# A cross-attention layer on one core: loads, roundings and query projections of the opening in another order

## The chip, the cores and the metric

The kernel runs on one core of one Trainium2 chip. The metric is the device time of one execution in microseconds, median of the runs. Before the change it is 512.16 us (three runs: 514.06, 511.97, 512.16).

## The reference, cut to what matters

```python
x = x + xattn(layernorm(x), ctx, mask)      # 128 queries, 12544 keys, 16 heads of 16, D = 256
x = x + attn(layernorm(x))                  # causal self-attention over the 128 rows
x = x + ffn(layernorm(x))                   # quantised gated MLP, 256 -> 768 -> 256

# xattn:
qh = (q @ Wq.T + bq).reshape(B, 128, 16, 16)
kh = (k @ Wk.T + bk).reshape(B, 12544, 16, 16)
vh = (v @ Wv.T + bv).reshape(B, 12544, 16, 16)
scores = einsum('bqhd,bkhd->bhqk', qh, kh) / 4
scores = where(mask, -1e7, scores)          # the mask of this case is all False
out = einsum('bhqk,bkhd->bqhd', softmax(scores), vh)
```

## The kernel before

The context has 14 blocks of 896 keys. A first phase (until about 243 us) goes through the blocks once: it projects keys and values, writes them to scratch in HBM, and finds each query's largest score. A second phase (until about 480 us) reads keys and values back, forms scores, exponentials and weighted sums. Self-attention and the MLP follow. The change is in the opening, the first 25 us or so, before the first phase has its rhythm.

Every fp32 operand of a key or value projection is kept as two parts, a rounded one and the rest: `ctx_hi` and `ctx_lo`, `w_hi` and `w_lo`. A projection is three products (hi x hi, hi x lo, lo x hi), each over two chunks of D: 6 matmuls for half a block of keys of one 128-row chunk (L815), 12 for two value tiles (L824).

Every engine has a program of its own, and their order is written by hand; semaphores tie them together. The parts that matter here:

- SyncE (SP) issues the loads one after another (L232 to L254): x, context block 0, Wk, Wv, the unit matrix `eye`, `wqn`, `bqn`, `head_mask`, `causal`, `bk`, and `mask_all`, the whole attention mask (1568 KB, L242). Then it waits until context block 0 is split, loads context block 1 into the same buffer (L245), and issues eight small loads for `bqr` and `row_mask` (L248 to L251), then `bv`, `wqvk`, `wo`, and the stores and loads of the block loop (L263, L265, L259).
- ScalarE (ACT) rounds context block 0 (L413, L414), spreads Wq's columns four-fold (L418, three copies), then evacuates keys (L427) and values (L433) in the order of the projections. Between two of these it rounds the next context block (L405), at position 5 of block 0 and position 3 of block 1. Later it also copies scores (L440, L443).
- VectorE (DVE) does the layer norm of x, rounds Wk and Wv into `w_hi` (L573), copies the turned rows (L567), forms `w_lo` (L575) and half of `ctx_lo` (L579), takes the projected queries out of PSUM (L595), forms `k_lo` of the first half block (L589), and writes `q_pad` (L599): for each of the 16 heads the 128 queries with all rows but this head's zeroed. Then `k_lo` of the second half, the maximum over the whole mask (L608), the flag "is anything masked" (L610), three casts of small matrices (`big_eye`, `eye_b`, `causal_b`, L612 to L614), four small steps on `row_mask` and `bqr` (L616 to L620), and `qr`, the spread queries with their bias (L621), which raises `q_copied`.
- GpSimd (POOL) forms the other half of `ctx_lo` (L359), issues two loads of mask rows (L356), fills `k_stack` with ones (L365), splits block 1 (L349, four pieces), waits for `q_copied`, and makes `q_stack` out of `qr` in eight operations (L370 to L377). Only then comes its share of block 2 (L349 again). SP loads a block into the single context buffer only after POOL has split the one before (L258, L259).
- TensorE (PE) first runs 14 matmuls on zeros (L867), then: transposes of x (L875), queries (L881), projections 0 and 2 of block 0, then 4 and 6 (`slot` counts in steps of two: keys 0/0, values 0, keys 0/1, values 1), the spread queries (L893, 32 matmuls into PSUM banks 2 and 3), the one-column sum of the flag (L898). It reads the flag (L900), branches (L1122), waits for `q_ready` and `q_copied` (L904, L905), and goes on with slot 8; from there every slot has a projection and one step of scores (L856).

```python
            pe.wait_ge(flag_ready, 1)
            masked_flag = pe.value_load(flag_i[0:1, 0:1], min_val=0, max_val=1)
            ...
                pe.wait_ge(q_ready, 1)
                pe.wait_ge(q_copied, 1)
```

The scores of step u go to banks 0 and 1 and, for even u, 2 and 3, for odd u, 4 and 5.

Of the kernel before, what the change touches and what calls it, by code (L numbers as in the profile page):

```python
# [4 lines left out]
H = 16  # L5
HD = 16
D = H * HD
Q = 128
SK = 12544
F = 768  # L10
P = 128
DC = D // P
# [34 lines left out]
WARM_FIRST = 14  # L47
# [4 lines left out]
def perceiver_layer(nc: bass.Bass, x_d, ctx_d, maskn_d, maskt_d, wqn_d, wqr_d, bqn_d, bqr_d, wk_d, bk_d, wv_d, bv_d,  # L52
# [9 lines left out]
    with ExitStack() as stack_of_contexts:  # L62
# [5 lines left out]
        def sem(name):  # L68
# [27 lines left out]
        q_pad = sb("q_pad", [P, H, Q], f32r)  # L96
# [33 lines left out]
        small = sb("small", [P, 16])  # L130
        magic = sb("magic", [P, 2])
# [98 lines left out]
        def _(sp):  # L230

            sp.dma_start(x0[:], x_d).then_inc(x_in, 16)  # L232
            sp.dma_start(ctx_t, ctx_d[0]).then_inc(ctx_in, 16)
            sp.dma_start(w_kv[:, 0:DC * D], wk_d.rearrange("p c n -> p (c n)")).then_inc(wkv_in, 16)
            sp.dma_start(w_kv[:, DC * D:], wv_d.rearrange("p c n -> p (c n)")).then_inc(wkv_in, 16)
            sp.dma_start(eye[:], eye_d).then_inc(eye_in, 16)
# [14 lines left out]
            sp.dma_start(row_mask[SLOTS::STRIDE, 2:4], pairmask_d[0:2 * HD, :]).then_inc(rows_in, 16)  # L251
            sp.dma_start(bv[:], bv_d).then_inc(bv_in, 16)
# [48 lines left out]
            sp.wait_ge(w_split, 1)  # L301
# [30 lines left out]
        def _(pool):  # L332
# [69 lines left out]
        def _(act):  # L402
# [11 lines left out]
            nc.scalar.copy(ctx_hi[:, 0, 1, :], ctx_t[:, BK:2 * BK]).then_inc(ctx_hi_ready, PIECES)  # L414
            act.wait_ge(wqn_in, 16)
# [29 lines left out]
            def evacuate(s, par, first, last=False):  # L445
# [3 lines left out]
                for slot, work in enumerate(PROJECTIONS):  # L449
# [92 lines left out]
        def _(dve):  # L542
# [22 lines left out]
            def copy_turned(nth, psum):  # L565
# [6 lines left out]
            dve.wait_ge(wkv_in, 32)  # L572
            link(nc.vector.tensor_copy(w_hi[:, :, :, :].rearrange("p w c n -> p (w c n)"), w_kv))  # L573
            copy_turned(1, ps_a[:, 0, 0:D])
            nc.vector.tensor_tensor(w_lo[:, :, :, :].rearrange("p w c n -> p (w c n)"), w_kv,  # L575
                                    w_hi[:, :, :, :].rearrange("p w c n -> p (w c n)").bitcast(f32),
                                    ALU.subtract).then_inc(w_split, 1)
            dve.wait_ge(ctx_hi_ready, 1)
            nc.vector.tensor_tensor(ctx_lo[:, 0, 1, :], ctx_t[:, BK:2 * BK], ctx_hi[:, 0, 1, :].bitcast(f32),  # L579
                                    ALU.subtract).then_inc(low_context, 1)  # L580
            dve.wait_ge(bq_in, 16)
# [10 lines left out]

            dve.wait_ge(q_projected, 1)
            for m in range(DC):
                link(nc.vector.tensor_scalar(x3[:, m * Q:(m + 1) * Q], ps_a[:, 1, m * Q:(m + 1) * Q], bqn[:, m:m + 1],  # L595
                                             HD ** -0.5, ALU.add, ALU.mult))
            low_keys(0, 0, 0, 0)
            for m in range(DC):
                last = nc.vector.tensor_tensor(  # L599
                    q_pad[:, m * HT:(m + 1) * HT, :],  # L600
                    x3[:, m * Q:(m + 1) * Q].unsqueeze(1).to_broadcast([P, HT, Q]),
                    head_mask[:, :].unsqueeze(2).to_broadcast([P, HT, Q]), ALU.mult)
# [582 lines left out]
```

## Time and profile before

| | us |
|---|---|
| median of three runs | 512.16 |
| the profiled execution | 513.95 |
| its span, first to last instruction | 512.2 |
| PE busy | 484.1 (95%) |
| ACT busy | 375.8 (73%) |
| DVE busy | 294.8 (58%) |
| POOL busy | 101.1 (20%) |
| mean granted TensorE clock | 0.966 of full speed |

Times in the profile count from the start of the span; 1.75 us of the profiled execution lie outside it. In the rows below, PE is matmuls and PEld weight loads; an engine's name with a q (SPq, PEldq) is its queue or sequencer. A weight load or matmul has the two halves of its name, out and in. Granted clock 1.00 is 2.4 GHz and 0.50 is 1.2 GHz.

### The profile page before, as it was taken

How to read it: one execution, taken by the hardware profiler on the slowest of the kernel's cores; microseconds unless marked ns; L12 is line 12 of the kernel's file. 1: busy time of each engine (PE TensorE's matmuls, PEld its weight loads, DVE VectorE, ACT ScalarE, POOL GpSimd, SP SyncE). 2: the span in 40 equal slices, each digit the busy share in tenths (PEclk: the TensorE clock that was granted, in tenths of full speed). 3: DMA queues.
4: the chain of work that ended last, by engine and by line, in shares of the span. 5: the costliest groups of instructions: out<-in, count | busy, mean ns of one | idle time of the engine just before them, and what ended most of it. 6: DMA issues, size and time to landing. Idle time of an engine off the chain costs nothing.

```text
span 512.2 us, 14299 instructions
## 1 busy us (share of the span) xinstructions
PE 484.1 (95%) x5643; PEld 380.3 (74%) x5643; DVE 294.8 (58%) x427; ACT 375.8 (73%) x411; POOL 101.1 (20%) x101
## 2 busy tenths in 40 slices
PE   6889999999999999996999999999999999989897
PEld 3867776777776777774489998999989999859443
DVE  6757999999999999999759600000000000046575
ACT  4347888888888788876389889899898999925011
POOL 5684322333322333304000000000000000000000
PEclk8879999999999999998799999999999999998799
DMA  8735776665776656985957788777677778000000
GB/s 275 262 123 210 284 282 267 236 233 229 300 289 257 242 219 240 388 349 213 385 188 288 302 309 307 275 252 274 259 268 271 273 292 312 3 2 1 0 0 14
DMA packets 34760, 117.47 MB, mean 229 GB/s; under 512 B 4401, under 2 KB 10417, under 8 KB 34737
## 3 DMA queue, kind: packets, MB, share of 16 engines
q1 hardware_dynamic: 30560, 110.58, 56.8%
q0 software_dynamic: 4032, 6.42, 4.4%
q8 instruction: 17, 0.28, 0.2%
q10 hardware_dynamic: 144, 0.13, 0.1%
q14 instruction: 7, 0.05, 0.0%
HBM read 74.44 MB, written 39.47 MB: 222 GB/s over the span
## 4 chain that ended last, share of the span: by engine, by line
PE 61%; DVE 22%; issue 8%; ACT 5%; DMA 2%; POOL 1%; DVEq 0%; SPq 0%; ACTq 0%; POOLq 0%
PE ps_a L953 20%; PE ps_k L967 18%; DVE block_max L628 10%; PE ps_k L815 6%; DVE early L631 5%; PE ps_a L824 4%; PE ps_a L856 3%; ACT early L443 3%; PE ps_k L867 2%; DMA early<-in_ctx 1%; DMA v_in<-in_wv 1%; DVE k_lo L589 1%; PE ps_a L1039 1%; PE ps_a L1054 1%; PE ps_a L893 1%
## 5 line engine op out<-in xcount | busy, mean ns | idle before, releaser
L628 DVE TENSOR_REDUCE block_max<-ps_a 128x2 f32<-128x896 f32 x112 | 120.8, 1080 | 1.8 <-PE ps_a L856 1.7
L953 PE MATMUL ps_a<-q_stack,k_stack 128*128 128x256 f32 x784 | 110.1, 291 | 1.4 <-ACT middle L494 1.4
L953 PEld LDWEIGHTS ps_a<-q_stack,k_stack 128*128 128x128 f32 x784 | 98.3, 188 | 13.5 <-issue 11.6
L443 ACT CAST early<-ps_a 128x896 bf16<-128x896 f32 x104 | 94.0, 903 | 8.0 <-PE ps_a L856 8.0
L494 ACT ACTIVATE middle<-ps_a 128x1536 f32<-128x1536 f32 (+1 forms) x56 | 90.2, 1662 | 10.6 <-PE ps_a L953 10.6
L494 ACT ACTIVATE early<-ps_a 128x1536 f32<-128x1536 f32 (+1 forms) x56 | 90.2, 1662 | 7.8 <-PE ps_a L953 7.8
L691 DVE COPY early<-ps_k 128x256 f32<-128x256 f32 x2 | 0.8, 420 | 163.7 <-PE ps_k L967 163.7
L349 POOL TENSOR_TENSOR k_stack<-early,k_stack 128x448 fp32r<-128x448 f32 x52 | 59.2, 1143 | 122.6 <-DVE early L631 113.6
L824 PE MATMUL ps_a<-w_hi,k_stack 128*128 128x256 f32 x392 | 69.8, 301 | 0.0
L631 DVE TENSOR_TENSOR early<-early 128x896 bf16<-128x896 bf16 x104 | 67.6, 650 | 0.0
L815 PE MATMUL ps_k<-k_stack,w_hi 128*128 128x448 f32 x224 | 61.8, 398 | 6.1 <-DVE v_in L621 3.9
L824 PEld LDWEIGHTS ps_a<-w_hi,k_stack 128*128 128x128 f32 x392 | 54.6, 194 | 11.9 <-issue 11.8
L856 PE MATMUL ps_a<-k_hi,q_pad 32*128 32x448 f32 x448 | 54.5, 475 | 8.6 <-ACT early L443 7.7
L427 ACT ACTIVATE k_hi<-ps_k,bk 128x448 fp32r<-128x448 f32 x56 | 35.6, 635 | 31.6 <-PE ps_k L815 31.6
L815 PEld LDWEIGHTS ps_k<-k_stack,w_hi 128*128 128x128 f32 x224 | 38.7, 192 | 20.9 <-DVE k_lo L589 11.0
L967 PE MATMUL ps_k<-early,v_in 128*17 128x128 f32 x1568 | 48.4, 273 | 0.0
L967 PE MATMUL ps_k<-middle,v_in 128*17 128x128 f32 x1568 | 48.2, 273 | 0.0
L856 PEld LDWEIGHTS ps_a<-k_hi,q_pad 32*128 32x128 f32 x448 | 22.0, 186 | 35.0 <-issue 23.6
L589 DVE SCALAR_TENSOR_TENSOR k_lo<-ps_k,bk,k_hi 128x448 fp32r<-128x448 f32 x56 | 38.0, 678 | 13.3 <-ACT k_hi L427 10.8
L967 PEld LDWEIGHTS ps_k<-early,v_in 128*17 128x17 f32 x1568 | 40.4, 97 | 3.9 <-ACT early L494 0.3
L967 PEld LDWEIGHTS ps_k<-middle,v_in 128*17 128x17 f32 x1568 | 40.4, 97 | 3.8
L433 ACT COPY early<-ps_a 128x512 f32<-128x512 f32 (+1 forms) x56 | 30.1, 537 | 15.2 <-PE ps_a L824 12.9
(172 smaller groups left out, 434.7 us busy)
## 6 DMA issues: line engine op xcount, KB each, us to landing
k_stack<-k_hi_scratch SPq DMA_DIRECT2D x56, 448.0 KB, 6.1
v_scratch<-early SPq DMA_DIRECT2D x14, 952.0 KB, 6.1
v_in<-v_scratch SPq DMA_DIRECT2D x14, 952.0 KB, 8.1
early<-in_ctx SPq DMA_DIRECT2D x14, 896.0 KB, 5.6
k_hi_scratch<-k_hi SPq DMA_DIRECT2D x28, 448.0 KB, 3.3
k_lo_scratch<-k_lo SPq DMA_DIRECT2D x28, 448.0 KB, 3.7
k_stack<-k_lo_scratch SPq DMA_DIRECT2D x28, 448.0 KB, 6.1
mask_b<-in_maskn POOLq DMA_DIRECT2D x14, 224.0 KB, 5.6
```

Source lines behind the costliest of these rows:

```text
L349: nc.gpsimd.tensor_tensor(ctx_lo[:, par, c, half], ctx_t[:, c * BK:(c + 1) * BK][:, half], ctx_hi[:, par, c, half].bitcast(f32), ALU.subtr ...
L427: nc.scalar.activation(k_hi[:, par, m, n * HK:(n + 1) * HK], ps_k[:, 0:HK], ACT.Identity, bias=bk[:, m:m + 1]).then_inc(hi_ready, 1)
L443: nc.scalar.copy(staged[:, u % 2], pair_scores(u, 0)).then_inc(max_copied, 1)
L494: nc.scalar.activation(probs[u % SLOTS_P][:, 0:width], ps_a[:, UNIT_BANK[u % 2]:UNIT_BANK[u % 2] + UP[u % 2] // 2, :].rearrange("p a n -> ...
L589: nc.vector.scalar_tensor_tensor(k_lo[:, m, half], ps_k[:, 0:HK], bk[:, m:m + 1], k_hi[:, par, m, half].bitcast(f32), ALU.add, ALU.subtrac ...
L628: nc.vector.tensor_reduce(block_max[:, par, 2 * u:2 * u + 2], pair_scores(u, 1), AX.X, ALU.max).then_inc(max_taken, 1)
L631: nc.vector.tensor_tensor(copied_rows(u), copied_rows(u), staged[:, u % 2], ALU.max).then_inc(run_taken, 1)
L815: last = nc.tensor.matmul(ps_k[:, 0:HK], w[:, 0, c, m * P:(m + 1) * P], part[:, par, c, n * HK:(n + 1) * HK], start=(k == 0), stop=(k == l ...
L824: last = nc.tensor.matmul(ps_v[:, n * D:(n + 1) * D], part[:, par, c, t * P:(t + 1) * P], w[:, 1, c, :], start=(j == 0), stop=(j == len(te ...
L856: last = nc.tensor.matmul(outs[-1], q_pad[rows, head, :], k_hi[rows, par, m, keys], start=True, stop=not masked, skip_group_check=True)
L953: last = nc.tensor.matmul(ps_a[:, bank, (k % 2) * 2 * Q:(k % 2 + 1) * 2 * Q], k_stack[:, b_par, a, t * P:(t + 1) * P], q_stack[:, a, :, :] ...
L967: last = nc.tensor.matmul(attended[32 * j:32 * j + VW, c * Q:(c + 1) * Q], v_ring[:, b_par, t, h, :], probs[slot][:, k * Q:(k + 1) * Q], s ...
```

## The change

SP: `eye` is loaded second, and the context, Wk and Wv behind it; Wk and Wv have a semaphore each. `causal` goes behind `mask_all`. The eight small loads go ahead of context block 1, and block 1 waits for `mask_all` to have landed as well. POOL issues the two loads of mask rows after filling `k_stack`, not before.

ACT rounds Wk and Wv, each when it is there, and makes `big_eye`, `eye_b` and `causal_b` after the evacuation of values 0. DVE forms `w_lo` in two halves, behind its half of `ctx_lo`. `q_pad` (16 heads x 128) becomes `q_pair` (2 x 2 x 128), the queries times a mask of two columns, even heads and odd heads; the score matmuls read 32 rows of it, which hold one head of each parity. The flag's sum goes to bank 3, and the spread queries to banks 4 and 5. PE: 12 zero matmuls and 6 more behind the transposes; spread queries between slots 2 and 4; slot 6 behind the flag's sum; `q_copied` is waited for before score step 1 and not ahead of slot 8.

```diff
-WARM_FIRST = 14
+WARM_FIRST = 12
+WARM_OPEN = 6
 @block.sync
             sp.dma_start(x0[:], x_d).then_inc(x_in, 16)
+            sp.dma_start(eye[:], eye_d).then_inc(eye_in, 16)
             sp.dma_start(ctx_t, ctx_d[0]).then_inc(ctx_in, 16)
-            sp.dma_start(w_kv[:, 0:DC * D], ...).then_inc(wkv_in, 16)
-            sp.dma_start(w_kv[:, DC * D:], ...).then_inc(wkv_in, 16)
-            sp.dma_start(eye[:], eye_d).then_inc(eye_in, 16)
+            sp.dma_start(w_kv[:, 0:DC * D], ...).then_inc(wk_in, 16)
+            sp.dma_start(w_kv[:, DC * D:], ...).then_inc(wv_in, 16)
...
-            sp.dma_start(causal[:], causal_d).then_inc(masks_in, 16)
             sp.dma_start(bk[:], bk_d).then_inc(bk_in, 16)
             sp.dma_start(mask_all...).then_inc(mask_all_in, 16)
-            sp.wait_ge(ctx_split, PIECES)
-            sp.wait_ge(low_context, 1)
-            sp.dma_start(ctx_t, ctx_d[1]).then_inc(ctx_in, 16)
+            sp.dma_start(causal[:], causal_d).then_inc(masks_in, 16)
             sp.wait_ge(row_mask_clear, 1)
             (eight small loads of bqr and row_mask)
+            sp.wait_ge(ctx_split, PIECES)
+            sp.wait_ge(low_context, 1)
+            sp.wait_ge(mask_all_in, 16)
+            sp.dma_start(ctx_t, ctx_d[1]).then_inc(ctx_in, 16)
 @block.gpsimd
-            load_rows(0, 0, True)
-            load_rows(1, 1, True)
             for n, (fill, value) in enumerate(fills[-2:]):
                 ...
+            load_rows(0, 0, True)
+            load_rows(1, 1, True)
 @block.scalar
+            for part, arrived in enumerate((wk_in, wv_in)):
+                act.wait_ge(arrived, 16)
+                nc.scalar.copy(w_hi[:, part]..., w_kv[:, part * DC * D:(part + 1) * DC * D]).then_inc(w_high, 1)
...
                         evacuate_values(s, par, work[1])
+                        if first and par == 0 and work[1] == 0:
+                            act.wait_ge(eye_in, 16)
+                            act.wait_ge(masks_in, 32)
+                            nc.scalar.mul(big_eye[:], eye[:], BIG).then_inc(eyes_set, 1)
+                            nc.scalar.copy(eye_b[:], eye[:]).then_inc(eyes_set, 1)
+                            nc.scalar.copy(causal_b[:], causal[:]).then_inc(eyes_set, 1)
 @block.vector
             layernorm(x0[:]).then_inc(normed, 1)
-            dve.wait_ge(wkv_in, 32)
-            link(nc.vector.tensor_copy(w_hi[...], w_kv))
             copy_turned(1, ps_a[:, 0, 0:D])
-            nc.vector.tensor_tensor(w_lo[...], w_kv, w_hi[...], ALU.subtract).then_inc(w_split, 1)
             (its half of ctx_lo)
+            for part in range(2):
+                dve.wait_ge(w_high, part + 1)
+                nc.vector.tensor_tensor(w_lo[:, part]..., ALU.subtract).then_inc(w_split, 1)
             dve.wait_ge(bq_in, 16)
             dve.wait_ge(masks_in, 32)
+            link(nc.vector.tensor_reduce(parity_mask[:], head_mask... "p (j e) -> p e j", AX.X, ALU.max))
             dve.wait_ge(q_projected, 1)
             (two steps L595)
+            nc.vector.tensor_tensor(q_pair[...], x3 to [P, 2, D], parity_mask to [P, 2, D], ALU.mult).then_inc(q_ready, 1)
             low_keys(0, 0, 0, 0)
-            (q_pad, two multiplications of 128x1024, then_inc(q_ready, 1))
-            low_keys(0, 0, 0, 1)
             nc.vector.memset(row_max[:], LEAST)
             dve.wait_ge(mask_all_in, 16)
             nc.vector.tensor_reduce(flag_f[:], mask_all, AX.X, ALU.max).then_inc(flag_asked, 1)
+            dve.wait_ge(rows_in, 16 * 2 * STRIDE)
+            (the scaling of bqr)
             dve.wait_ge(flag_summed, 1)
+            (flag_i, out of bank 3).then_inc(flag_ready, 1)
-            (big_eye, eye_b, causal_b; the wait for rows_in)
+            low_keys(0, 0, 0, 1)
+            dve.wait_ge(q_projected, 2)
             (three steps on row_mask, then qr).then_inc(q_copied, 1)
 @block.tensor
+                if isinstance(s, int) and s * NG + u == 1:
+                    pe.wait_ge(q_copied, 1)
...
             last.then_inc(transposed, 1)
+            keep_clock(ps_v, WARM_OPEN)
...
-            pe.wait_ge(w_split, 1)
             pe.wait_ge(ctx_split, PIECES)
             pe.wait_ge(low_context, 1)
-            for slot in range(H - 2 * LAG):
-                project(0, 0, slot)
+            pe.wait_ge(w_split, 1)
+            project(0, 0, 0)
+            pe.wait_ge(w_split, 2)
+            project(0, 0, 2)
             pe.wait_ge(wq_spread, 3)
             (spread queries, into ps_a banks 4 and 5 in place of 2 and 3)
+            project(0, 0, 4)
             pe.wait_ge(flag_asked, 1)
             (the flag's sum, bank 3 in place of 5)
+            project(0, 0, 6)
             pe.wait_ge(flag_ready, 1)
             masked_flag = pe.value_load(...)
...
                 pe.wait_ge(q_ready, 1)
-                pe.wait_ge(q_copied, 1)
+                pe.wait_ge(eyes_set, 3)
```

## Rows read from the trace of the kernel before

**Rows 1.** Stretch; us; busy PE, PEld, DVE, ACT, POOL; clock; DMA share; GB/s.
```profile
8.00:12.00 4.00, 2.05 (x10) 1.81 (x10) 3.96 (x4) 2.08 (x3) 3.69 (x4) 0.75 1.03 316
17.00:26.90 9.90, 6.68 (x55) 6.37 (x54) 9.00 (x14) 3.28 (x4) 4.43 (x5) 1.00 0.71 223
27.20:33.80 6.60, 6.20 (x26) 4.90 (x26) 1.99 (x3) 1.58 (x3) 6.01 (x5) 0.50 0.31 123
45.00:220.00 175.00, 169.46 (x1119) 124.92 (x1120) 172.05 (x239) 146.42 (x228) 60.14 (x60) 1.00 0.70 266
```

**Rows 2.** The chain that ended last, in the opening: start us, us, what.
```profile
7.54 2.25 DVE w_hi L573
...
10.24 1.13 DVE w_lo L575
11.37 1.01 DVE k_stack L579
...
12.52 2.58 PE ps_k L815 x6
...
18.57 1.42 PE ps_a L824 x12
19.99 3.57 PE ps_a L893 x32
...
26.28 1.24 DVE v_in L621
...
27.60 2.58 PE ps_k L815 x6
```

**Rows 3.** Timeline: first matmuls of slot 12 and of two key slots behind.
```profile
34.15 1.08 PE L815 MATMUL ps_k<-k_stack,w_hi 128*128 128x448 f32 x4
...
37.55 1.08 PE L815 MATMUL ps_k<-k_stack,w_hi 128*128 128x448 f32 x4
...
41.40 0.47 PE L815 MATMUL ps_k<-k_stack,w_hi 128*128 128x448 f32 x1
```

**Rows 4.** Timeline, POOL and DVE; in brackets the idle time before.
```profile
7.16 2.07 POOL L359 TENSOR_TENSOR k_stack<-early,k_stack 128x896 fp32r<-128x896 f32 x1 [4.75 <-ACT k_stack L413]
...
12.51 0.74 DVE L595 TENSOR_SCALAR x<-ps_a,bqn 128x128 f32<-128x128 f32 x2
...
16.57 2.35 DVE L599 TENSOR_TENSOR q_pad<-x,head_mask 128x1024 fp32r<-128x1024 f32 x2
...
19.27 0.68 DVE L589 SCALAR_TENSOR_TENSOR k_lo<-ps_k,bk,k_hi 128x448 fp32r<-128x448 f32 x1 [0.34 <-ACT k_hi L427]
...
19.90 3.40 DVE L608 TENSOR_REDUCE flag_f<-middle 128x1 f32<-128x3136 int32 x1
...
23.72 0.15 DVE L610 TENSOR_SCALAR flag_i<-ps_a 1x1 int32<-1x1 f32 x1 [0.42 <-PE ps_a L898]
```

**Rows 5.** The large mask's load L242: duration ns, start us; issue to landing, us.
```profile
L242 SPq DMA_DIRECT2D middle<-in_maskn x1: 439/439/439, 6.0 to 6.0; - x1
...
DMA to landing us min/median/max: 10.7/10.7/10.7
```

**Rows 6.** The last step of PE's reading of the flag, in its sequencer.
```profile
L900 PEldq SEQ_ASSERT  x1: 32/32/32, 24.7 to 24.7; - x1
```

**Rows 7.** The twelve context loads of L259: issue to landing, us.
```profile
DMA to landing us min/median/max: 4.7/5.6/6.9
```

**Rows 8.** Timeline: rounding of block 1, end of `q_stack`, block 2, load and use of block 3.
```profile
19.14 1.68 ACT L405 CAST k_stack<-early 128x1792 fp32r<-128x1792 f32 x1
...
36.87 2.39 POOL L377 TENSOR_TENSOR q_stack<-q_stack,v_in 128x1024 fp32r<-128x1024 f32 x1
...
44.26 4.45 POOL L349 TENSOR_TENSOR k_stack<-early,k_stack 128x448 fp32r<-128x448 f32 x4 [5.01 <-ACT k_stack L405]
...
48.88 0.36 SPq L259 DMA_DIRECT2D early<-in_ctx  x1
...
55.97 0.58 ACT L410 CAST k_stack<-early 128x448 fp32r<-128x448 f32 x1
```

More of the change, by code:

```diff
@@ L95, in perceiver_layer @@
         w_kv = v_in[:, 2 * PR * Q:2 * PR * Q + 2 * DC * D]
-        q_pad = sb("q_pad", [P, H, Q], f32r)
+        q_pair = sb("q_pair", [P, 2, DC, Q], f32r)
         q_stack = sb("q_stack", [P, PR, 2, Q], f32r)
@@ L414, in _ @@
             nc.scalar.copy(ctx_hi[:, 0, 1, :], ctx_t[:, BK:2 * BK]).then_inc(ctx_hi_ready, PIECES)
+            for part, arrived in enumerate((wk_in, wv_in)):
+                act.wait_ge(arrived, 16)
+                nc.scalar.copy(w_hi[:, part].rearrange("p c n -> p (c n)"),
+                               w_kv[:, part * DC * D:(part + 1) * DC * D]).then_inc(w_high, 1)
             act.wait_ge(wqn_in, 16)
@@ L580, in _ @@
                                     ALU.subtract).then_inc(low_context, 1)
+            for part in range(2):
+                dve.wait_ge(w_high, part + 1)
+                nc.vector.tensor_tensor(w_lo[:, part].rearrange("p c n -> p (c n)"), w_kv[:, part * DC * D:(part + 1) * DC * D],
+                                        w_hi[:, part].rearrange("p c n -> p (c n)").bitcast(f32),
+                                        ALU.subtract).then_inc(w_split, 1)
             dve.wait_ge(bq_in, 16)
@@ L596, in _ @@
                                              HD ** -0.5, ALU.add, ALU.mult))
+            nc.vector.tensor_tensor(q_pair[:, :, :, :].rearrange("p e m q -> p e (m q)"),
+                                    x3[:, :].unsqueeze(1).to_broadcast([P, 2, D]),
+                                    parity_mask[:, :].unsqueeze(2).to_broadcast([P, 2, D]), ALU.mult).then_inc(q_ready, 1)
             low_keys(0, 0, 0, 0)
[L598 to L602, printed above, removed]
-            last.then_inc(q_ready, 1)
-            low_keys(0, 0, 0, 1)
             nc.vector.memset(row_max[:], LEAST)
@@ L608, in _ @@
             nc.vector.tensor_reduce(flag_f[:], mask_all, AX.X, ALU.max).then_inc(flag_asked, 1)
+            dve.wait_ge(rows_in, 16 * 2 * STRIDE)
+            link(nc.vector.tensor_scalar(bqr[:], bqr[:], HD ** -0.5, None, ALU.mult))
             dve.wait_ge(flag_summed, 1)
-            nc.vector.tensor_scalar(flag_i[0:1, 0:1], ps_a[0:1, 5, 0:1], 0.0, None, ALU.is_gt).then_inc(flag_ready, 1)
-            dve.wait_ge(eye_in, 16)
-            nc.vector.tensor_scalar(big_eye[:], eye[:], BIG, None, ALU.mult)
-            nc.vector.tensor_copy(eye_b[:], eye[:])
-            nc.vector.tensor_copy(causal_b[:], causal[:])
-            dve.wait_ge(rows_in, 16 * 2 * STRIDE)
+            nc.vector.tensor_scalar(flag_i[0:1, 0:1], ps_a[0:1, 3, 0:1], 0.0, None, ALU.is_gt).then_inc(flag_ready, 1)
+            low_keys(0, 0, 0, 1)
+            dve.wait_ge(q_projected, 2)
             link(nc.vector.tensor_tensor(row_mask[:, 4:6], row_mask[:, 0:4:2], row_mask[:, 1:4:2], ALU.add))
@@ L855, in score_for_max @@
                         outs.append(pair_scores(u, w)[:, at, :])
-                        last = nc.tensor.matmul(outs[-1], q_pad[rows, head, :], k_hi[rows, par, m, keys],
+                        last = nc.tensor.matmul(outs[-1], q_pair[rows, head % 2, m, :], k_hi[rows, par, m, keys],
                                                 start=True, stop=not masked, skip_group_check=True)
@@ L892, in _ @@
                 for c in range(DC):
-                    last = nc.tensor.matmul(ps_a[:, 2 + a // 4, (a % 4) * Q:(a % 4 + 1) * Q], wq_rows(c, a, a + 1), xt[:, c, :],
+                    last = nc.tensor.matmul(ps_a[:, 4 + a // 4, (a % 4) * Q:(a % 4 + 1) * Q], wq_rows(c, a, a + 1), xt[:, c, :],
                                             start=(c == 0), stop=(c == DC - 1))
             last.then_inc(q_projected, 1)
+            project(0, 0, 4)
             pe.wait_ge(flag_asked, 1)
-            nc.tensor.matmul(ps_a[0:1, 5, 0:1], flag_f[:], ones_c[:], start=True, stop=True).then_inc(flag_summed, 1)
+            nc.tensor.matmul(ps_a[0:1, 3, 0:1], flag_f[:], ones_c[:], start=True, stop=True).then_inc(flag_summed, 1)
+            project(0, 0, 6)
             pe.wait_ge(flag_ready, 1)
```

21 lines of the change are left out of this document (9 added, 12 removed).

## The prediction, made before the changed kernel was run

> **What bounds the kernel now.** I read the busy times by stretch first. Between 45 and 220 us DVE is busy 172.05 of 175 us and PE 169.46, at full clock [rows 1]: a rhythm of matmuls and maxima with hardly a hole. Nothing of it is changed: the score matmuls read `q_pair` in place of `q_pad`, at the same shape, 32 rows by 128. So the change is worth how much earlier this rhythm starts, unless something late in the opening holds it back.
>
> The second view is the chain of waits in the opening [rows 2]. It is one string. DVE rounds the weights (2.25 us from 7.54), copies the turned rows, forms `w_lo` (1.13) and half of `ctx_lo` (1.01); at 12.52 PE starts the first projection. Four projections and the spread queries run to 23.56. Then PE stops: it does the flag's sum, and its next matmul is at 27.60. In between DVE has the flag, three casts, small steps and `qr` (26.28, 1.24 us), and PE waits for `q_copied` ahead of slot 8.
>
> The third view is the clock. In 17 to 26.9 us the granted clock was full (2.4 GHz), and PE was busy 6.68 of 9.90 us; from 27.2 to 33.8, after PE had stood still since about 23.7, it was half (1.2 GHz), with PE busy 6.20 of 6.60 [rows 1]. So the stop costs twice. Slots 8 and 10 with their score steps took 27.60 to 34.15, 6.55 us; a later pair of a key slot and a value slot took 37.55 to 41.40, 3.85 us [rows 2, 3]. 2.7 us are the price of the low clock.
>
> **The change, part by part.**
>
> *Start of PE's projections.* ACT takes the rounding, so DVE's 2.25 us go. That piece was long because of a neighbour: it ended at 9.79, 0.56 us after POOL's subtraction did (7.16 + 2.07 = 9.23) [rows 2, 4]. In the new order DVE's half of `ctx_lo` (1.01) stands beside that same subtraction. Block 0's own load is issued one place later, some 0.4 us (an issue is 439 ns [rows 5]), so `ctx_lo` is ready at about 9.4 if the two don't disturb each other and at 10.5 if DVE is held until POOL is done. `w_lo` is two halves of some 0.6 (1.13 / 2), so slot 0 starts between 10.0 and 11.1. I take 11.1, since the one row of two such neighbours shows the hold; before it was 12.52. `eye` arrives early, so the transposes don't wait for it. The six added zero matmuls lie in the time in which DVE copies and `wqn` arrives: nothing; uncovered, no more than six matmuls of 448 columns at half clock, 2.58 [rows 2].
>
> *DVE's gate.* Most rests on this step. DVE still waits for `masks_in` = 32 ahead of taking the queries, and `causal`, one of its two loads, is now issued behind `mask_all`, 1568 KB. So DVE stands from about 11.7 until the mask has passed. Before, the mask was issued at 6.0 and landed 10.7 later, at 16.7 [rows 5], with two mask-row loads of POOL and context block 1 beside it. In 8 to 12 us the queues moved 316 GB/s at a busy share of 1.03 [rows 1]: 1264 thousand bytes, nearly all of it this mask. The rest of its 1606, 342, takes 1.1 us at that rate: 13.1. Now nothing runs beside it, and it is issued one place sooner. Bounds: 12.6, and 16.2 (as before, less that place). I take 13.3 for mask and `causal`, nearer to the rate, since the companions of its tail are gone.
>
> *DVE behind the gate.* Two-column reduction 0.2 (an estimate: L610, as small, took 0.15), queries out of PSUM 0.74, `q_pair` 0.6 for 512 columns in place of 2.35 for 2048, `k_lo` 0.68, memset and gap 0.1, the reduction over the mask 3.40 [rows 4]: 13.3 + 5.7 = 19.0. Then 0.42 until PE's sum is there and 0.15 for the flag: 19.6. `k_lo` of the second half 0.7, to 20.3; three steps on `row_mask` 0.6 (0.2 each); `qr` 1.24: `q_copied` at 22.1. The scaling of `bqr` lies in the 0.42. The eight small loads for it stand directly behind the mask in the queue and are needed only at 19.0: free; if they were late to 20, as much is added. The three casts leave DVE for ACT, which has nothing to do between values 0 (14.6) and the keys of slot 4 (18.9): free, as long as `causal` comes before; without that cover they would hold the evacuation of slot 4 by their own length, 1 us or so.
>
> *PE.* Slot 0 from 11.1, at full clock 1.4 each for slots 0 and 2 (1.42 for slot 6), spread queries 3.57 [rows 2]: 17.5; slot 4 to 18.9; flag's sum at 19.1; slot 6 from 19.3 to 20.7. If the clock were half for slot 0, as at 12.52 where it took 2.58, slots 0 and 2 are late by some 2.5; 0.2 of that is room before 19.1, and the flag and all behind it wait for the rest at most.
>
> *The branch.* Reading the flag and branching lay under the wait for `q_copied`: from the flag's 23.87 to past 24.7 [rows 4, 6], 0.9 and the branch. Now PE has them bare, or they run while slot 6's matmuls are still in the array: 0 to 1.0; I take 0.5. Slot 8 then starts at 21.3 (before: 27.60). It also needs `k_lo` of 20.3, which is there. Score step 0 is at 22.8, step 1 at 24.7, and its new wait for `q_copied` (22.1) is met with 2.6 us to spare; were it not, slot 12 and all of PE would stand behind it. Slots 8 and 10 at full clock take 3.85: slot 12 starts at 25.15, before at 34.15 [rows 3]. **9.0 us earlier.**
>
> *What is late next.* Context block 1 now waits for the mask: issued at 13.4, where before it went behind `ctx_lo` at 12.4 [rows 2]. POOL's two mask-row loads run beside it, later than before, since the fills are ahead of them. With 4.7 to 6.9 us to landing [rows 7] it is there at 18.1 to 20.3; ACT wants it at 19.6, after the keys of slot 4. POOL's order is fixed: split of block 1 (4.45, as for block 2), `q_stack` from 27.6 to 39.3, that is 11.7, then block 2, which it began at 44.26 after 5.01 us of idleness [rows 8]. Now: landing 19.2 (the middle), ACT 1.7, POOL 4.5 and 11.7: block 2 at 37.1, where 35.3 would keep the whole 9.0 (44.26 - 9.0). POOL is 1.8 late. Load 3 follows that split: before it was issued at 48.88 and used at 55.97 [rows 8], 7.1 later, where a load needs 5.6 [rows 7]. That slack of 1.5 takes most of it; 0.3 to 0.4 are lost. **Gain of the profiled execution 8.6: 513.95 - 8.6 = 505.35** (span 512.2, and 1.75 outside it, which stay).
>
> *From the profiled execution to the median.* It stood 1.8 over the median (513.95 against 512.16). The low clock is worth 2.7, and I can't see whether the timed runs had it; the 1.8 speaks for some without. I credit half, 1.35: gain 7.25, time **504.9**.
>
> A rule of the Trainium skill bears on the start: GpSimd shares its SBUF interfaces with VectorE, "contention with DVE instructions in a 2-port perf mode or with two SBUF inputs" ("GPSIMD Engine Reference", section "8. Key points"). The trace agrees for the cast, 2.25 us beside POOL's subtraction. By the rule the start of slot 0 is held to 11.1, without it 10.0; the sum is the same by both here, since DVE stands at its gate until 13.3.
>
> **The rivals.** Each is a loss against the gain of 7.25.
>
> A. *The gate opens late.* The mask keeps its tail and lands at 16.2. For it: it came at 16.7, though the rate would have had it through long before. Against: the tail had other loads beside it. DVE's chain and the load of block 1 move by 2.9. Gain 4.35: 507.8.
>
> B. *The clock stays down or falls.* For it: PE stands between 8 and 11 us, and again for about 0.4 at 18.9 and 0.5 at the branch; the mean clock of 0.75 in 8 to 12 [rows 1] is half of that stretch at half. If slots 8 and 10 run at half, 2.7 don't come; if slots 0 and 2 do, 2.3. Against: PE is busy nearly all of 11 to 19, and it kept full clock at 6.68 of 9.90. Gain about 4.7: 507.5.
>
> The Trainium skill holds that the array is throttled by default and activity releases it ("TensorE: Matmul & The Clock Gate", section "What's actually happening"). The trace agrees: full clock stands behind a stretch of work, half behind a stop.
>
> C. *The load chain decides.* Block 1 lands at 20.3 to 21, not 19.2: POOL is another 1.1 to 1.8 late, with the slack in load 3 used up. Gain 5.4 to 6.1: about 506.4.
>
> D. *The other side: block 1 comes so late that the opening is longer than before.* SP issues it only behind `mask_all`; ACT, in order, stands at its rounding with the evacuations of slots 6 and 8 queued behind; and 17.9 us (1.7 + 4.5 + 11.7) lie between landing and POOL's block 2. It decides from a landing at 44.26 - 17.9 + 1.5 = 27.9; at 29 it costs 1.1: 513.3. For it: the mask alone took 10.7. Against: 14.5 from issue to landing have no row; the longest context load took 6.9.
>
> E. *The change doesn't do what it says*: the spread queries are not behind the flag but in its way, and slot 8's path still ends in `qr`. Then slot 8 starts no sooner than 22.1 + 1.0, 1.8 less: 506.7.
>
> **How the numbers follow.** Forecast with its own spread (gate 12.6 to 14.5, branch 0 to 1, clock credit 0 to 2.7: 503.0 to 506.4) 0.60; A 0.13, B 0.11, C 0.07, E 0.04, D 0.05. A and B end near 508, both together at 510.3. Range 502.3 to 508.5, which leaves out D, A with B, and a little below. Runs of this kernel can tell about 0.5%, 2.6 us, from no change. Faster than 509.6: 0.91; same: 0.04 (the part of A and B in which both come); slower: 0.05 (D).
>
> **What would show it.** The mask and `causal` landing together at about 13.3, DVE idle from about 11.7 until then; the reduction over the mask from about 15.6; slot 8 at about 21.3 with granted clock 1.00; slot 12 at 25.2; POOL with little idle time between its split of block 1, `q_stack` and block 2; the rhythm after 45 us unchanged in its pace. The prediction is wrong if the gate opens after 15, if the granted clock is 0.50 in 21 to 25 us, or if ACT waits for context block 3 by more than 1 us.

## The result, and the profile after

The changed kernel takes 507.88 us (median of six, 506.0 to 511.89), the kernel before 512.4 in the same comparison; the ratio of the runs is 0.9925, with a 95% interval of 0.9896 to 0.9954. So it is faster, by 0.75%. Forecast were 504.9 us, a gain of 7.25 us; the ratio stands for 3.8. Direction and range held, the size didn't: about half of the gain came. The profiled execution took 511.06, near the long end of the six; its forecast was 505.35, a gain of 8.6 us, and 2.9 came. The mean granted clock is 0.983 in the shortest of the six and 0.973 in the two longest.

The chain that ended last, after (start us, us, what; compare [rows 2]):

```profile
8.78 2.34 DVE k_stack L588
...
11.87 2.58 PE ps_k L823 x6
...
16.14 3.57 PE ps_a L905 x32
...
21.50 1.69 ACT k_stack L409
...
23.27 4.46 POOL k_stack L353 x4
...
37.01 2.39 POOL q_stack L381
...
45.26 6.58 DMA early<-in_ctx
```

Before, the chain of the opening was PE and DVE in all the rows of [rows 2]. Now from 21.5 on it is ACT's rounding of block 1, POOL's split, `q_stack`, the split of block 2, and the load of block 3. The timeline of the same kernel, with the engines' wait in brackets (compare [rows 3, 4, 8]):

```profile
13.88 0.16 DVE L607 TENSOR_REDUCE parity_mask<-head_mask 128x2 f32<-128x8 f32 x1 [1.55 <-DMA causal<-in_causal]
...
16.07 3.40 DVE L619 TENSOR_REDUCE flag_f<-middle 128x1 f32<-128x3136 int32 x1
...
21.16 0.15 DVE L623 TENSOR_SCALAR flag_i<-ps_a 1x1 int32<-1x1 f32 x1 [1.61 <-PE ps_a L910]
...
22.50 1.03 PE L823 MATMUL ps_k<-k_stack,w_hi 128*128 128x448 f32 x4
...
26.28 1.08 PE L823 MATMUL ps_k<-k_stack,w_hi 128*128 128x448 f32 x4
...
29.67 1.07 PE L823 MATMUL ps_k<-k_stack,w_hi 128*128 128x448 f32 x4
...
39.75 5.34 POOL L353 TENSOR_TENSOR k_stack<-early,k_stack 128x448 fp32r<-128x448 f32 x4 [0.36 <-POOL q_stack L381]
...
45.26 0.36 SPq L263 DMA_DIRECT2D early<-in_ctx  x1
...
51.87 0.56 ACT L414 CAST k_stack<-early 128x448 fp32r<-128x448 f32 x1 [3.68 <-DMA early<-in_ctx]
```

Slot 12 starts at 26.28, 7.9 us before that of [rows 3]; forecast were 9.0. The last row is where it is lost: ACT waits 3.68 us for context block 3, and PE behind it. The prediction had named a wait of more than 1 us there as a sign that it is wrong. By stretch (columns as in [rows 1]):

```profile
17.00:26.90 9.90, 9.90 (x74) 8.55 (x73) 7.17 (x11) 5.41 (x9) 4.66 (x6) 1.00 0.81 305
27.20:33.80 6.60, 6.39 (x44) 4.54 (x43) 4.82 (x7) 4.80 (x9) 6.42 (x6) 1.00 0.71 195
45.00:220.00 175.00, 166.68 (x1086) 123.21 (x1087) 167.44 (x233) 142.53 (x222) 56.61 (x57) 0.98 0.71 266
48.20:52.40 4.20, 2.35 (x15) 1.58 (x13) 2.69 (x4) 0.54 (x2) 0.00 (x0) 1.00 1.05 331
52.50:59.20 6.70, 5.35 (x23) 4.28 (x24) 3.85 (x6) 5.12 (x9) 3.40 (x3) 0.50 0.79 327
```

From 17 us on the opening has the shape of the forecast, 1.1 us late: PE without a hole from 17 to 26.9, and full clock in 27.2 to 33.8. Then PE is busy 2.35 of 4.20 us while block 3 is awaited, and the clock is granted at half in 52.5 to 59.2, a second price.

One measure for all kernels here: the start of VectorE's n-th maximum of the first phase (L628 before, L636 after; 112 of them, eight a block), as a lead in us over the kernel before. A column is the first maximum of its block; in block 0 it is the last, and so it is in block 13.

```
kernel                        block 0  block 1  block 2  block 3  block 12  block 13 (end)
changed                          7.9      7.9      2.9      2.7      2.6       2.6
before, zero matmuls             2.5      2.5      2.5      2.5      2.5       2.5
before, q_stack late             0.3      0.3      0.3      0.3      0.2      -5.9
changed, q_stack late            8.9      9.0      9.0      9.0      9.0       3.1
changed, no q_stack              8.1      8.1      8.1      8.1      8.1       8.1
changed, early rounding          7.3      7.3      7.3      7.3      7.3       7.3
changed, ctx_lo on DVE           9.3      9.3      6.6      6.3      6.3       6.3
changed, q_copied waited early   6.4      6.4      6.2      6.1      6.1       6.1
changed, block 1 loaded first    7.5      7.5      2.5      2.3      2.3       2.3
changed, causal first            8.7      8.7      3.4      3.2      3.2       3.2
changed, no open matmuls         7.3      7.3      2.3      2.1      2.1       2.1
early rounding + ctx_lo          7.6      7.6      7.6      7.5      7.5       7.5
best version                     9.8      9.8      9.8      9.8      9.7       9.7
```

The changed kernel has its lead whole until the sixth maximum of block 1, loses 5.0 us from there to the start of block 2, and next to nothing after that. So the loss is one event.

Each row is a single execution, set against a single one of the kernel before, which took 513.95 us where its median is 512.4: read the leads for where time is lost, and the ratios for how much. At least two things differ between the executions without an edit that explains them. The clock in 11 to 15 us, in which slots 0 and 2 run, was full in seven of the ten traces that have the six zero matmuls, and at half for most of it in three: the changed kernel, `q_copied` waited early, and block 1 loaded first. And in the self-attention, long after the opening, it was at half for some 3 us in the kernel before and full in the same work of others (columns as in [rows 1]):

```profile
459.00:464.00 5.00, 4.47 (x23) 4.24 (x24) 2.40 (x4) 0.37 (x1) 0.00 (x0) 0.66 0.00 0
```

```profile
459.00:464.00 5.00, 4.93 (x40) 4.59 (x40) 4.42 (x7) 2.06 (x6) 0.00 (x0) 1.00 0.00 0
```

The first is the kernel before, the second the kernel before with zero matmuls (below): its lead goes from 2.5 to 3.9 us there.

### The profile page after: what moved, and what is told of

Read it like the earlier page. It is cut to its first block, busy times and chain, and to the rows that moved or that the text cites. A ratio compares the mean times of both kernels' runs of the same rounds, so it can differ in the third digit from the quotient of the medians.

```text
span 509.4 us, 14309 instructions
## 1 busy us (share of the span) xinstructions
PE 480.5 (94%) x5647; PEld 378.2 (74%) x5647; DVE 290.6 (57%) x424; ACT 377.4 (74%) x416; POOL 102.2 (20%) x101
## 4 chain that ended last, share of the span: by engine, by line
PE 53%; DVE 27%; issue 10%; POOL 4%; ACT 3%; DMA 2%; DVEq 1%; SPq 0%; POOLq 0%; ACTq 0%
PE ps_a L967 20%; PE ps_k L981 18%; DVE block_max L636 13%; DVE early L639 7%; PE ps_k L823 3%; DMA early<-in_ctx 2%; PE ps_a L832 2%; DVE k_lo L603 2%; POOL k_stack L353 2%; ACT early L451 1%; PE ps_a L866 1%; PE ps_a L877 1%; POOL q_stack L381 1%; PE ps_a L1053 1%; DVE early L664 1%
## 5 line engine op out<-in xcount | busy, mean ns | idle before, releaser
L636 DVE TENSOR_REDUCE block_max<-ps_a 128x2 f32<-128x896 f32 x112 | 120.8, 1080 | 1.4 <-PE ps_a L866 1.2
L508 ACT ACTIVATE middle<-ps_a 128x1536 f32<-128x1536 f32 (+1 forms) x56 | 90.2, 1663 | 10.6 <-PE ps_a L967 10.6
L866 PE MATMUL ps_a<-k_hi,q_pair 32*128 32x448 f32 x448 | 54.7, 477 | 11.7 <-ACT early L451 11.0
L866 PEld LDWEIGHTS ps_a<-k_hi,q_pair 32*128 32x128 f32 x448 | 22.0, 186 | 37.9 <-issue 26.1
L981 PEld LDWEIGHTS ps_k<-early,v_in 128*17 128x17 f32 x1568 | 40.4, 97 | 4.0 <-ACT early L508 0.3
L981 PEld LDWEIGHTS ps_k<-middle,v_in 128*17 128x17 f32 x1568 | 40.4, 97 | 3.8
```

The costliest lines, as they stand in the source:

```text
L508: nc.scalar.activation(probs[u % SLOTS_P][:, 0:width], ps_a[:, UNIT_BANK[u % 2]:UNIT_BANK[u % 2] + UP[u % 2] // 2, :].rearrange("p a n -> ...
L636: nc.vector.tensor_reduce(block_max[:, par, 2 * u:2 * u + 2], pair_scores(u, 1), AX.X, ALU.max).then_inc(max_taken, 1)
L866: last = nc.tensor.matmul(outs[-1], q_pair[rows, head % 2, m, :], k_hi[rows, par, m, keys], start=True, stop=not masked, skip_group_check= ...
L981: last = nc.tensor.matmul(attended[32 * j:32 * j + VW, c * Q:(c + 1) * Q], v_ring[:, b_par, t, h, :], probs[slot][:, k * Q:(k + 1) * Q], s ...
```

## The experiments

Theory 1: POOL's fixed order (split of block 1, `q_stack`, split of block 2) decides when block 3 can be loaded, and that took the missing part of the gain. Rivals: the load is slow by itself; the lead is lost in the loop whatever feeds it; the new order of loads is to blame.

**q_stack behind the block loop, on the changed kernel.**

```diff
-            pool.wait_ge(q_copied, 1)
-            for ab in range(2):   (the eight operations)
             with pool.Fori(1, NB // 2) as i:
                 ...
+            pool.wait_ge(q_copied, 1)
+            for ab in range(2):   (the eight operations)
```

> The changed kernel with POOL's eight q_stack operations (11.7 us) moved behind the block loop; nothing else. Theory 1 (POOL's order decides: split of block 1, q_stack, split of block 2, then load 3): POOL splits block 2 as soon as ACT has rounded it at 36.2, done at about 41, load 3 issued at 41 and there at 47.5, ahead of ACT's wish at 48.2; ACT's wait for load 3 goes from 3.7 us to 0, the granted clock stays 1.00 at 52 to 59 us, and DVE keeps its lead of 7.9 us over the kernel before to the end: profiled execution about 505.8, ratio to before 0.984 to 0.987. Rival (load 3 is slow by itself, landing 6.6 us because of other transfers): the wait stays at 1 us or more and the ratio stays at 0.990 to 0.9925. Rival (the lead is lost in the loop whatever feeds it): DVE's lead falls to 2.6 at block 2 again.

Measured: 511.3 us, ratio 0.999 (0.9972 to 1.0009). In the loop theory 1 held: load 3 issued at 39.9, no wait, lead 9.0 from block 1 to block 12, full clock. But the ratio that I expected didn't come: at block 12, where the moved operations now ran, 5.8 us went.

The lead was expected at 7.9. It is 9.0 because slots 0 and 2 had the full clock in this execution: slot 4 starts at 18.21, slot 8 at 21.40 and slot 12 at 25.21, where 25.15 was forecast for the changed kernel.

**The same move on the kernel before.**

> The kernel before with the same move of q_stack behind the block loop. Theory 1: before, POOL stood idle for 5.0 us ahead of block 2 and load 3 had slack; nothing is won, ratio 0.998 to 1.002. Rival (q_stack disturbs DVE or the loads by running beside them, and its place matters by itself): ratio 0.996 or less.

Measured: 520.17 us, ratio 1.015 (1.0122 to 1.0177). Lead 0.3 until block 12, so its place in the loop indeed won nothing there; then 6.2 us lost. The ratio stands for 7.7 us; where the rest goes isn't located. The expected ratio failed for the same reason, which the timeline shows:

```profile
218.65 1.13 POOL L375 TENSOR_SCALAR q_stack<-v_in,row_mask 128x1024 fp32r<-128x1024 f32 x1
218.69 3.75 DVE L631 TENSOR_TENSOR early<-early 128x896 bf16<-128x896 bf16 x1
```

And all such passes of 215 to 232 us, by line (ns min/median/max), first this kernel, then the kernel before without the move:

```profile
L631 DVE TENSOR_TENSOR early<-early x7: 609/1019/3746, 214.5 to 230.9; 128x896 bf16<-128x896 bf16 x7
```

```profile
L631 DVE TENSOR_TENSOR early<-early x10: 609/610/778, 214.7 to 231.4; 128x896 bf16<-128x896 bf16 x10
```

A two-input pass of VectorE that takes 0.61 us took 3.75 beside back-to-back passes of POOL. Theory 2: VectorE's two-input passes are held while POOL works. This is the rule of the Trainium skill that the prediction cited ("GPSIMD Engine Reference", section "8. Key points"), here with a price. The old place of `q_stack` is harmless because VectorE has none of these passes until the maxima of block 1 (the first pass is at 41.9 in the changed kernel), when `q_stack` is done.

**No q_stack at all:**

```diff
+            nc.gpsimd.memset(q_stack[...], 0.0)      # ahead of the split of block 1
-            for ab in range(2):   (the eight operations)
+            nc.gpsimd.memset(q_stack[:, 0, 0, 0:1], 0.0).then_inc(q_spread, 8)
```

> The changed kernel without the arithmetic of q_stack: POOL fills q_stack with zeros while it waits for context block 1, and in place of the eight operations of 11.7 us does one tiny fill. Left out: the spread queries of the second phase, so its scores are wrong. Theory 1 (POOL's order decides load 3): as q_stack moved away in the loop, and without the operations that stood beside VectorE at block 12: ACT does not wait for load 3, DVE's lead over the kernel before is 7.5 to 9 us at block 2 and stays so to block 13, ratio 0.981 to 0.986. Theory 2, on the failure of the late q_stack (GpSimd's two-input and other passes hold VectorE's L639, one took 3.75 us for 0.61): with no such pass at block 12 the 5.7 us lost there don't appear. Rival to theory 2 (block 12 loses time because the phase ends earlier or the clock falls there by itself): the lead falls by 4 us or more at block 12 here too.

Measured: 505.51 us, ratio 0.9849 (0.9817 to 0.988), lead 8.1 to the end of the first phase, nothing lost at block 12. Both theories held; the ratio lies inside what was expected. The clock in 11 to 15 us was full here; that it isn't what kept the lead is shown by `causal` ahead of the mask (below), which had full clock there too, kept `q_stack`, and waited 3.85 us for block 3.

**Block 1 rounded ahead of slot 4's evacuation**, POOL's order untouched:

```diff
-PREPARE_SLOTS = (5, 3)
+PREPARE_SLOTS = (3, 3)
```

> The changed kernel with ACT rounding block 1 ahead of the evacuation of slot 4 (PREPARE_SLOTS 3, 3) instead of behind it; POOL's order as it is. Block 1 had landed at 19.1, ACT began at 21.5. Theory 1: everything of POOL moves by 2.4 us: split of block 1 at 20.9, block 2 at 37.4, load 3 at 42.9, there at 49.5, ACT's wait falls from 3.7 to 1.3 us; PE stands too briefly for the clock to fall, so lead after block 2 about 6.5 and ratio 0.986 to 0.988. Rival (POOL's split is bound by DVE's maxima, its four pieces took 5.3 us for 4.45): gain under 1 us, ratio 0.990 or more.

Measured: 505.42 us, ratio 0.9869 (0.984 to 0.9898), lead 7.3 throughout. The timeline, with block 1's rounding, block 2's split, and load and use of block 3:

```profile
19.92 1.69 ACT L409 CAST k_stack<-early 128x1792 fp32r<-128x1792 f32 x1 [3.81 <-DMA early<-in_ctx]
...
38.21 4.47 POOL L353 TENSOR_TENSOR k_stack<-early,k_stack 128x448 fp32r<-128x448 f32 x4 [0.36 <-ACT early L448]
...
42.84 0.36 SPq L263 DMA_DIRECT2D early<-in_ctx  x1
...
48.63 0.58 ACT L414 CAST k_stack<-early 128x448 fp32r<-128x448 f32 x1
```

Rounding 1.6 us sooner made load 3 2.4 us sooner, since the split also was 4.47 us and not 5.34; ACT didn't wait at all, where I had expected 1.3 us.

Not all of the 1.6 us is the edit's. With the full clock in 11 to 15 us that this execution had, ACT reached the rounding at 20.25 in the version with `q_stack` late and at 20.85 with `causal` first, both in the old order. And the edit costs something in the opening: slot 4's keys stand behind the rounding, slot 12 starts at 26.82, and ACT wants block 3 only at 48.6. The load itself took 5.2 us and not 6.6. The lead is kept by all of these together.

**Both halves of block 0's `ctx_lo` on DVE**, POOL's subtraction out, a test of theory 2:

```diff
-            pool.wait_ge(high_chunk, 1)
-            nc.gpsimd.tensor_tensor(ctx_lo[:, 0, 0, :], ...).then_inc(ctx_split, PIECES)
+            dve.wait_ge(high_chunk, 1)
+            nc.vector.tensor_tensor(ctx_lo[:, 0, 0, :], ...).then_inc(ctx_split, PIECES)
```

> The changed kernel with both halves of ctx_lo of block 0 on DVE, POOL's subtraction taken out. Theory 2 (DVE's two-input pass was held by POOL's: 2.34 us for 896 columns where 1.09 was seen alone): DVE's halves take about 1.0 each, 8.0 to 10.0, w_lo at 10.6, so slot 0 starts at 10.6 to 10.8 and not 11.9, though DVE does twice the work; slot 12 about 1 us sooner; POOL's chain 1 us sooner too, so ACT waits for load 3 by 2.7 and not 3.7 us. Rival (2.34 us is the price of reading beside the running loads or ACT): the two halves take 3 to 4.6 us and slot 0 starts at 12.5 or later.

```profile
7.76 1.09 DVE L585 TENSOR_TENSOR k_stack<-early,k_stack 128x896 fp32r<-128x896 f32 x1 [0.36 <-ACT k_stack L414]
8.77 1.08 DVE L588 TENSOR_TENSOR k_stack<-early,k_stack 128x896 fp32r<-128x896 f32 x1
```

Both halves take 2.17 us on DVE; half of them took 2.34 beside POOL. Slot 0 starts at 10.6 in place of 11.87. Measured 507.29, ratio 0.9893 (0.9856 to 0.9929): the lead rises to 9.3, stands at 9.1 within block 1, and 2.8 of it go at block 3's load, which is still late. ACT waits 2.27 us for it, though it had rounded block 1 at 19.3, as soon as that had landed: POOL's order makes the load late even when the rounding is not.

**`causal` ahead of the mask:**

```diff
+            sp.dma_start(causal[:], causal_d).then_inc(masks_in, 16)
             sp.dma_start(bk[:], bk_d).then_inc(bk_in, 16)
             sp.dma_start(mask_all...)
-            sp.dma_start(causal[:], causal_d).then_inc(masks_in, 16)
```

> The changed kernel with the load of causal ahead of bk and the mask, as it was. The prediction's gate (DVE waits for causal behind the mask, to 13.9 us) opens at 9 to 10 us. If the gate decides the opening: the reduction over the mask starts at the mask's landing, 13.6, and not 16.1, the flag is out 1.5 to 2.5 us sooner and so is slot 12. If PE decides it (its slot 4 ended at 20.95 and the flag's sum stood behind it, DVE waited 1.6 us for PE): slot 12 at 26.3 within 0.3 us, ratio 0.990 to 0.9935 as without the edit, because load 3 also stays late.

Measured: 510.11, ratio 0.9945 (0.9918 to 0.9971), no better than the changed kernel. DVE passed its gate at 12.8 without a wait, but the reduction over the mask started at 15.7 in place of 16.1, since the mask itself, issued 1.1 us later, landed 2.1 us later:

```profile
15.68 3.42 DVE L619 TENSOR_REDUCE flag_f<-middle 128x1 f32<-128x3136 int32 x1 [0.27 <-DMA middle<-in_maskn]
```

Slot 12 came 0.8 us sooner, in a profiled execution with full clock in 11 to 15 us, where the changed kernel's had half; with full clock and the gate as it was, `q_stack` late has it at 25.21, 0.3 sooner still. So the edit won nothing in the opening. Load 3 was late as ever: ACT waited 3.85 us.

**`q_copied` waited for ahead of slot 8 again**, one part undone:

```diff
-                if isinstance(s, int) and s * NG + u == 1:
-                    pe.wait_ge(q_copied, 1)
+                pe.wait_ge(q_copied, 1)          # behind eyes_set, as before
```

> The changed kernel with the wait for q_copied put back ahead of slot 8 (one part of the change undone). q_copied came at 24.0 and slot 8 started at 22.5, so PE stands 1.5 us and slot 12 starts at 27.8 in place of 26.3. Theory 1 (POOL's chain to load 3 decides, not PE's start): POOL's chain hangs on ACT's rounding of block 1 and q_copied, neither moves, so load 3 is issued at 45.3 as without the edit; ACT's wait for it shrinks from 3.7 to about 2.2 us and the lead from block 3 on is the same 2.6 within 0.5 (better by up to 1.5 if the shorter stop spares the clock): ratio 0.989 to 0.993, no slower than the changed kernel. Rival (PE's start decides and passes on): ratio 1.5 us worse, 0.995 or more.

Measured: 507.32 us, ratio 0.9888 (0.9866 to 0.9911), no slower than the changed kernel with its 0.9925. Slot 8 starts 1.4 us later, and the lead at block 1 is 6.4; 6.1 of it stay. So PE's earlier start isn't worth anything while load 3 decides. The expectation was wrong in part: load 3 was issued at 44.0, not 45.3, ACT waited 0.1 us and not 2.2, and the kept lead is larger (6.1 and not 2.6 to 4.1). DVE's passes and POOL's split of block 2 were less in each other's way (4.46 us, not 5.34), and the load took 5.7 us and not 6.6.

**Block 1 loaded ahead of the small loads and without its wait for the mask**, another part undone:

> The changed kernel with the load of context block 1 back ahead of the eight small loads and without its wait for the mask (another part undone). It is issued at 10.5 to 11 and not 14.2, and lands at 16.5 to 18. ACT rounds it at 21.5 as before, since it stands behind the evacuation of slot 4, so by theory 1 nothing of POOL's chain moves: load 3 late as it was, ratio 0.990 to 0.994. Rival (the new order of loads delays block 1 and so load 3): load 3 issued 2 us or more sooner, ratio 0.988 or less. A cost is possible: the mask shares the queue with block 1 and the flag comes up to 1.5 us later.

Measured: 507.75, ratio 0.9894 (0.9874 to 0.9914); in the profiled execution load 3 is issued at 45.6 and the lead falls to 2.3, as in the changed kernel. There the new order of loads is not to blame: block 1 lands at 16.7, and ACT rounds it at 21.9, behind slot 4. The ratio lies a little below the expected 0.990 to 0.994, its interval overlaps that of the changed kernel, and the profiled execution is the longest of the seven: that the order costs nothing over the runs is not shown.

**Without the six zero matmuls:**

> The changed kernel without the six matmuls on zeros behind the transposes. If they hold the clock up: the granted clock is 0.50 for more of 10 to 17 us, and slot 4 and slot 12 come up to 2 us later; by theory 1 load 3 then is up to 2 us later too (ACT rounds block 1 behind slot 4), ratio 0.993 to 0.997. If they do nothing: slot 12 at 26.3 within 0.5 and ratio 0.990 to 0.9935.

Measured: 511.75 us, ratio 0.9981 (0.9966 to 0.9997), so nearly all of the gain over the runs. In the profiled execution the clock was half in 8.7 to 15.5 us, slot 4 started 0.6 us later, and the lead fell to 2.1 at block 3's load. That is 0.6 us against the changed kernel's profiled execution, where the ratios stand 0.56% apart; but all twelve runs lie at 510.8 to 512.5, while four of the changed kernel's six lie at 506 to 508.1. I take it that the matmuls decide in how many runs slots 0 and 2 get the full clock and the opening is early enough for load 3 to be met; the traces of the other runs, which would show it, I don't have.

**The low clock alone, on the kernel before:**

```diff
                 pe.wait_ge(q_ready, 1)
+                keep_clock(ps_a[:, 0, :], 10)
                 pe.wait_ge(q_copied, 1)
```

> The kernel before with ten matmuls on zeros between PE's branch and its wait for q_copied, 24.9 to 27.1 us, into a PSUM bank that nothing reads; no other edit. If the low clock of 27 to 34 us is a cost of PE's stop: granted clock 1.00 there, slots 8 and 10 take 3.9 us and not 6.55, and since POOL had 5 us and load 3 1.5 us of room before, all 2.7 stay to the end in the profiled execution; over the runs, half or more of it, ratio 0.9945 to 0.998. Rival (the low clock hits only some runs, the profiled one among them): ratio 0.998 to 1.000. Rival (the gained time is lost at load 3 as in the changed kernel): lead 2.7 at block 1, under 1 from block 2.

```profile
27.20:33.80 6.60, 6.60 (x42) 4.61 (x41) 3.33 (x4) 3.45 (x6) 5.76 (x5) 1.00 0.40 140
```

Full clock in the stretch in which [rows 1] has half. Slots 8 and 10 take 27.81 to 31.66, 3.85 us; lead 2.5 to the end of the first phase; 509.91 us, ratio 0.9967 (0.9946 to 0.9989), 1.7 us. The 2.7 us are borne out by the 2.5 of the lead. The profiled execution as a whole is 4.0 us shorter; 1.3 of that is the clock in the self-attention. The half credited to the median, 1.35, fits the ratio, whose interval runs from 0.6 to 2.8 us.

**Early rounding and `ctx_lo` on DVE together:**

> Both together on the changed kernel: block 1 rounded ahead of slot 4's evacuation, and both halves of block 0's ctx_lo on DVE. If the two gains add: lead at block 1 8.3 to 9, no wait for load 3, ratio 0.983 to 0.986. If the start of PE is not what sets slot 12 (DVE's chain behind the mask takes over, slack 1.6 us): lead as with the early rounding alone, 7.3, ratio 0.9865 to 0.988.

Measured: 505.61, ratio 0.9852 (0.982 to 0.9884), lead 7.5: in the lead the gains don't add, though the ratio lies where it was expected if they do. Block 1 lands at 19.7, and ACT, waiting for it, lets the keys of slot 4 (done at about 19) stand until 21.3; slot 8 starts at 22.8. So block 1 must land sooner.

**The best version:** these two, `causal` ahead of the mask, and block 1 loaded ahead of the small loads and without the wait for the mask.

> Early rounding of block 1, both halves of block 0's ctx_lo on DVE, block 1 loaded ahead of the small loads and without waiting for the mask, causal ahead of the mask. Theory 1: block 1 is there at 17 to 18, ACT rounds it before slot 4's keys are done (18.2), so it no longer holds up slot 8 as it did in the version with the first two edits (slot 8 at 22.8, lead 7.5); lead 9 to 9.5 with no wait for load 3, profiled execution about 503 to 504.5, ratio 0.981 to 0.985. Rival (the mask's share of the queue makes the flag late, or block 1 lands at 19.7 all the same): lead 7 to 8, ratio 0.985 to 0.987.

```profile
17.46 1.69 ACT L405 CAST k_stack<-early 128x1792 fp32r<-128x1792 f32 x1 [2.35 <-DMA early<-in_ctx]
```

Measured: 503.97 us (503.6 to 504.3), ratio 0.9827 (0.9805 to 0.9849). Slot 8 starts at 20.55, load 3 is issued at 40.4, ACT does not wait for it, and the lead of 9.7 reaches the end. It beats both kernels.

## Why the prediction was half right

*Start of PE's projections*: slot 0 at 11.87 (forecast 11.1). The hold by POOL was real: 2.34 us for DVE's half. "The sum is the same by both", as the prediction had it, is nearly so: with the full clock, slot 0 at 12.01 and at 10.60 give slot 12 at 25.21 and at 24.82.

*DVE's gate*: the mask landed at 13.6 and `causal` at 13.8, forecast 13.3; issue and landing of the mask, to compare with [rows 5]:

```profile
L244 SPq DMA_DIRECT2D middle<-in_maskn x1: 434/434/434, 5.4 to 5.4; - x1
...
DMA to landing us min/median/max: 8.1/8.1/8.1
```

So rival A was out, and the rate was the right guide. Whether most rests on this gate hangs on the clock: in this trace DVE waited 1.55 us there and then 1.61 for PE's flag sum, so PE decided; with full clock in 11 to 15 us (`q_stack` late) it was 1.49 at the gate and 0.28 for the sum. The experiment that opened the gate won nothing that shows over the runs, since the mask then landed later.

*DVE behind the gate*: 5.6 us to the end of the reduction, forecast 5.7. *PE*: slots 0 and 2 ran at half clock until 14.9 (the case of rival B, in part), 4.3 us for 2.8, so slot 4 started at 19.47 and not 17.5. The six zero matmuls, which the prediction put at nothing, bear on this: without them the clock was at half from 8.7 to 15.5, and nearly all of the gain over the runs was gone. *The branch*: slot 8 at 22.50, with no gap behind slot 6; reading the flag was hidden under it, the lower end of 0 to 1.0. *Slots 8 and 10*: 3.78 us, forecast 3.85. Together slot 12 was 1.1 us late, 26.28 for 25.15; in the trace with full clock it was at 25.21.

**The step that failed is "What is late next"**: 0.3 to 0.4 us lost at block 3 were forecast, and 5.3 were lost in the profiled execution. Its mechanism was right, and is now shown; its sizes were not, and it had no term for the clock. By its terms block 3 was usable at 37.1 + 4.5 + 5.6, 47.3 with the issue; it was 51.87. The 4.5 us are 2.65 + 0.85 + 1.0:

- POOL's split of block 2 started at 39.75 and not 37.1. The sum took the landing of block 1 (forecast 19.2, measured 14.20 + 4.9 = 19.1) for the start of its rounding. But ACT rounds it behind slot 4's keys, at 21.50. With the rounding moved ahead of slot 4 the lead was kept (0.9869 over the runs), but this alone doesn't decide: with `ctx_lo` on DVE the rounding began at 19.3, right at the landing, and ACT still waited 2.27 us. Some 1.2 us of the late start are the half clock's: with the full clock the rounding began at 20.25.
- The split took 5.34 and not 4.45 us, beside DVE's two-input passes.
- Block 3's load took 6.6 and not 5.6 us; it was issued just ahead of the stores of block 1's keys and values. In all five traces in which the first of these stores follows 0.6 us behind load 3, the load takes 6.45 to 6.74 us; in the nine in which 1.6 us or more lie between, 5.0 to 5.7. So a load late enough to meet the stores was later by another 1 us; no experiment moved the stores alone.

ACT wanted block 3 at 48.2, so it waited 3.7, and PE stood long enough for the clock to fall: the lead went from 7.9 to 2.6, 1.5 of it after ACT had its data (51.87 was 4.1 ahead of the 55.97 of [rows 8]). Rival C was this mechanism, with 1.1 to 1.8 us and without the clock; but its condition, block 1 landing at 20.3 to 21, didn't come: it landed at 19.1. Rivals D and E didn't occur.

*The median*: its gain of 3.8 to 4.5 us stands over the 2.9 of the profiled execution. The mean clocks of the six runs (0.973 to 0.983) fit a stop at block 3 that is met in some runs and not in others; that is argued from the clocks, not shown. That the median lies within the range is in part luck: none of the rivals held a stop at block 3 of this size.

## What to carry to other kernels

When an opening gets shorter, follow every in-order engine to the first transfer that hangs on it in the new order, and start its sum where that engine gets to the work, not where the data lands. A load that has just enough room may have none once it meets other transfers. An engine that is 20% busy can still decide, by a handful of operations that nobody needs yet. And moving such operations to an idle stretch of their own engine can cost more than it frees: they must lie where the neighbour has none of the passes that they hold, as VectorE has none here while `q_stack` is made at its old place, 27.7 to 39.4 us.

## What the runs showed of the hardware that I had not expected

VectorE's two-input bf16 maximum of 896 columns, 0.61 us alone, took 3.75 us beside back-to-back single-input passes of POOL: not a slowdown but a stop until POOL had done three of them. It goes the other way too: POOL's pass of 128x448, 1.15 us, took 1.59 when DVE's pass had begun 0.03 us before it (at 41.9 in the changed kernel). A fill of POOL held no such pass: DVE's half of `ctx_lo` took 1.01 us [rows 2] beside a fill that ran from 10.78 to 13.89. And six matmuls on zeros, 1.5 us of PE's time, were worth 0.5% over the runs, though the profiled execution without them was only 0.6 us behind.
